# Ordering the last attention group by tile of queries, and starting each tile's output, norm and logits among the rest

## What is computed

```python
q, k, v = (split_heads(x @ W + b) for W, b in ((Wq, bq), (Wk, bk), (Wv, bv)))
attn = einsum('bhqd,bhkd->bhqk', q, k) / sqrt(32) + alibi        # causal mask
out = einsum('bhqk,bhkd->bhqd', softmax(attn), v) @ Wo + bo
x1 = layernorm(x + out)
logits = x1 @ Wr + br                                            # 4 experts, top 1
y = (silu(x1 @ Wg[e]) * (x1 @ Wu[e])) @ Wd[e] * top_w            # e: the expert of the token
result = layernorm(x1 + y)
```

## Time and profile before

| what | value |
|---|---|
| median of 3 runs | 1259.69 us (1257.77 to 1263.88) |
| the profiled execution | 1257.54 us, span 1255.8 us |
| PE busy | 1165.1 us, 93% of the span |
| DVE, ACT, POOL busy | 61%, 45%, 24% |
| first score of the last group (unit 180) | 451.13 us |
| last product with values (unit 191) | 483.97 us |
| o63 done | 486.37 us |
| routing starts on DVE | 509.53 us |

### The profile page before, as it was taken

One profiled execution on the slowest core, in us unless ns is written; L12 is line 12 of the kernel. 1 busy time (PEld: TensorE's weight loads), 2 busy tenths in 40 slices (PEclk: granted clock), 3 DMA queues, 4 the chain that ended last, 5 costly groups with the idle time before them and its releaser, 6 DMA issues.

```text
span 1255.8 us, 27816 instructions
## 1 busy us (share of the span) xinstructions
PE 1165.1 (93%) x8697; PEld 1063.2 (85%) x8697; DVE 768.6 (61%) x1978; ACT 570.4 (45%) x1395; POOL 307.3 (24%) x443
## 2 busy tenths in 40 slices
PE   6998998999899987499999999999999999999994
PEld 5888888887888875498998899899989988998993
DVE  3676767676767776456546655664665465456665
ACT  4676766765666673043323332332333232323344
POOL 5400201201020122353213311330331133123336
PEclk9999999999999998589999999999999999999997
DMA  8223223222322240271322223122313222231302
GB/s 274 62 52 79 71 67 103 54 60 68 94 52 64 68 123 35 61 200 44 93 68 62 75 79 91 51 85 68 93 51 91 72 60 76 72 98 51 85 33 103
DMA packets 109685, 100.11 MB, mean 80 GB/s; under 512 B 12847, under 2 KB 81839, under 8 KB 109552
## 3 DMA queue, kind: packets, MB, share of 16 engines
q1 hardware_dynamic: 104784, 87.85, 24.8%
q0 software_dynamic: 3040, 9.18, 2.2%
q10 hardware_dynamic: 1728, 1.31, 0.3%
HBM read 64.74 MB, written 9.18 MB: 59 GB/s over the span
## 4 chain that ended last, share of the span: by engine, by line
PE 76%; DVE 6%; POOL 5%; ACT 4%; issue 4%; DMA 3%; SPq 1%; ACTq 0%; DVEq 0%; POOLq 0%
PE bank L805 35%; PE bank L583 14%; PE bank L830 10%; PE bank L721 4%; PE bank L704 4%; POOL up_lo L1455 4%; PE bank L817 3%; PE bank L693 2%; DMA up_raw<-in_Wu_dram 2%; SPq L475 1%; ACT probs L913 1%; DVE probs L1153 1%; PE bank L730 1%; PE bank L681 1%; ACT up_hi L945 1%
## 5 line engine op out<-in xcount | busy, mean ns | idle before, releaser
L805 PE MATMUL bank<-up_hi,xsT_hi 128*128 x1216 | 356.2, 293 | 5.7 <-POOL up_lo L1455 4.6
L805 PE MATMUL bank<-up_lo,xsT_hi 128*128 x1216 | 344.6, 283 | 0.0
L805 PE MATMUL bank<-up_hi,xsT_lo 128*128 x1216 | 344.5, 283 | 0.0
L1455 POOL TENSOR_TENSOR up_lo<-up_raw,up_hi 128x256 fp32r<-128x256 f32 x241 | 169.9, 741 | 477.8 <-ACT up_hi L945 477.6
L1294 DVE SCALAR_TENSOR_TENSOR h_tok<-bank,row_weight,silu 128x128 f32<-128x128 f32 x304 | 93.4, 347 | 292.3 <-ACT silu L1009 292.3
L805 PEld LDWEIGHTS bank<-up_hi,xsT_hi 128*128 128x128 f32 x1216 | 233.0, 192 | 12.3 <-issue 12.0
L805 PEld LDWEIGHTS bank<-up_hi,xsT_lo 128*128 128x128 f32 x1216 | 233.7, 192 | 0.3
L805 PEld LDWEIGHTS bank<-up_lo,xsT_hi 128*128 128x128 f32 x1216 | 233.1, 192 | 0.0
L1009 ACT ACTIVATE silu<-bank 128x256 f32<-128x256 f32 (+1 forms) x160 | 59.6, 373 | 364.5 <-PE bank L805 364.5
L1311 DVE TENSOR_TENSOR y<-bank,y 128x512 f32<-128x512 f32 x295 | 198.5, 688 | 0.5
L913 ACT ACTIVATE probs<-probs,neg_max 128x512 f32<-128x512 f32 (+3 forms) x256 | 136.5, 558 | 56.4 <-DVE neg_max L1153 55.4
(11 more groups left out here) (168 smaller groups left out, 2083.8 us busy)
## 6 DMA issues: line engine op xcount, KB each, us to landing
up_raw<-in_Wg_dram SPq DMA_DIRECT2D x64, 256.0 KB, 3.5
up_raw<-in_Wu_dram SPq DMA_DIRECT2D x64, 256.0 KB, 4.1
down_raw<-in_Wd_dram SPq DMA_DIRECT2D x64, 256.0 KB, 2.7
k_stack<-qk_hi SPq DMA_DIRECT2D x128, 64.0 KB, 2.0
q_stack<-qk_hi SPq DMA_DIRECT2D x128, 64.0 KB, 2.0
k_stack<-qk_lo SPq DMA_DIRECT2D x64, 64.0 KB, 2.0
q_stack<-qk_lo SPq DMA_DIRECT2D x64, 64.0 KB, 2.0
x_tok<-in_x_dram SPq DMA_DIRECT2D x3, 1024.0 KB, 5.5
```

The source lines that it names most:

```text
L805: mm = pe.matmul(bank[:, n * 2 * P:(n + 1) * 2 * P], a[:, s, k, :], up_w[w][k][:, :, :].rearrange("p a f -> p (a f)")[:, bass.ds(at, 2 * P ...
L1455: pool.tensor_tensor(up_w[1][k][:, e, :], up_raw[:, idx % NUPS, k, :, :].rearrange("p g f -> p (g f)"), up_w[0][k][:, e, :].bitcast(F32), ...
```

## The change

The last group (heads 60 to 63) is no longer ordered by head but by tile of queries, in the order 2, 1, 3, 0. A "head" of that group now means one tile for all four heads: tile 2 is four units of 3 blocks, tile 1 two units of 4 blocks, tile 3 four units of 4 blocks, tile 0 one unit of 4 blocks. That makes 11 units instead of 12, with the same 40 blocks; `U` is 191. The first four units (180 to 183) each take another head's stack. Each `o6x` now completes one tile's rows, so `OT_last`, `OP_rest`, the norm and the logits of a tile become jobs of the plan, which runs on to unit 204 (`plan.units`) for them. `OT_last` is four jobs with 128 columns instead of one with 512. Two splits of expert weights on ACT (`split_up`), which stood behind the loop, go to units 195 and 196 (`UP_AT`). Up to unit 179 no instruction moves, and SP's list is the same throughout.

```diff
+TILE_ORDER = (2, 1, 3, 0)
+TILE_UNITS = {0: ((0, 1, 2, 3),), 1: ((0, 1), (2, 3)), 2: ((0,), (1,), (2,), (3,)), 3: ((0,), (1,), (2,), (3,))}
+UNITS = [(g, g * GH + h, [(h, i) for i in tiles]) for g in range(NG - 1) for h in range(GH) for tiles in UNIT_TILES]
+UNITS += [(NG - 1, (NG - 1) * GH + n, [(h, i) for h in heads]) for n, i in enumerate(TILE_ORDER) for heads in TILE_UNITS[i]]
...
+ROWS = list(range(T0)) + [T0 + i for i in TILE_ORDER]
...
+UP_AT = {U + VLAG + n: NUPS + n for n in range(NE - NUPS)}
...
+        if kind == "OT_last":
+            return [("o", DONE + LAST * NH + ROW[t] - T0), ("read", "OP", NT - 1)]
+        if kind == "x1t":
+            return [("ln", t)] + ([("read", "logit", ROWS[ROW[t] - 2])] if t >= T0 else [])
...
+                for job in list(queue) if u >= U else [queue[0]]:
+                    if all(k in ready for k in needs(job)):
+                        break
...
+                for t in ROWS[T0:]:
+                    queue.extend((kind, t) for kind in ("OT_last", "OP_rest", "x1t", "logit"))
...
-                if u % PER_HEAD == 0:
-                    pe.wait_ge(s_stack[h], stack_count(g))
+                for n, h, i, at, width in spans(pairs):
+                    if n == 0 and u % PER_HEAD == 0 and g < NG - 1 or g == NG - 1 and END[g * GH] >= u:
+                        pe.wait_ge(s_stack[h], stack_count(g))
...
-            head_values(NB * NH - 1)
-            for job in plan.after_loop + plan.tail:
-                side(job, 0, len(cost_of(job)))
...
-            for job in plan.after_loop + plan.tail[0:1 + QT]:
-                take(job)
-            for e in range(NUPS, NE):
-                split_up(0, e)
-            for job in plan.tail[1 + QT:]:
-                take(job)
+                if u in UP_AT:
+                    split_up(0, UP_AT[u])
...
-            for t in range(T0, NT):
-                take(("OP_rest", t))
-                moments(t)
-                if t > T0:
-                    normalise(t - 1)
-            normalise(NT - 1)
```

More of the change, by code:

```diff
@@ L98, in cost_of @@
             "OT": [53] * (3 if t // QT == LAST else 4), "OP": [213] * (9 if t // QT == LAST else 12),
[L99 removed]
+            "x1t": [53] * 4, "logit": [107] * 8, "OT_last": [53], "OP_rest": [213] * 3}[kind]
 class Plan:
@@ L106, in __init__, with next_bank, add @@
         self.number, self.bank, self.before, self.act_number = {}, {}, {}, {}
[L107 to L110, removed]
+        self.slices, self.taken_at = defaultdict(list), defaultdict(list)
+        self.moments_at, self.normal_at = {}, {}
         self.flushed = {}
         self.used = {}
[L114 to L118, removed]
+    def next_bank(self, banks):
+        return min(range(banks), key=lambda n: self.number.get(self.used.get(n), 0))
+    def add(self, job, bank):
+        self.number[job] = len(self.number) + 1
         self.bank[job] = bank
@@ L187, in owed @@
         return sum(c for _, c in left) + sum(sum(cost_of(j)) for j in queue)
-    for u in range(U + VLAG):
+    u = 0
+    while u < U + VLAG + 4 or queue or left or pending or later:
         flush(u)
+        if u == U:
+            for bank in range(2, 6):
+                plan.used.pop(bank, None)
         if u in SPLIT_BY:
@@ L541, in sync @@
             x_due = 2
-            for u in range(U + VLAG):
+            for u in range(plan.units):
                 if x_due <= NB and plan.flushed.get(("OP", (x_due - 2) * QT + QT - 1), U + 9) <= u:
@@ L697, in unit_transpose @@
             def unit_transpose(u):
-                blocks = sum(i + 1 for i in UNITS[u][2])
                 bank = banks[2 + u % 2]
@@ L1214, in step @@
                 dve.wait_ge(s_route, steps[0])
-            dve.wait_ge(s_side_dve, done("logit", NT - 1))
+            dve.wait_ge(s_side_dve, max(done("logit", t) for t in range(NT)))
             step(dve.tensor_reduce(mx, logits[:, :, :], AX_X, ALU.max))
```

211 lines of the change are left out of this document (102 added, 109 removed).

## The result

The changed kernel takes 1263.9 us (median of 20 runs, 1259.35 to 1268.38), the kernel before 1260.91 us in the same measurement (20 runs, 1257.77 to 1264.52). The ratio is 1.0027, with a 95% interval of 1.0014 to 1.0039: slower by 2 to 5 us, and less than the 0.5% that I called a difference. The forecast was 1264.5. It came so near the 1263.9 partly by luck: it was built on the 1259.69 us of three runs, and the 20 runs put the kernel before 1.2 us higher. The difference was forecast as 4.9 us, and the medians differ by 3.0.

What follows compares the result with a forecast made beforehand. Behind the last product, latency of a chain through all engines was the bound. A walk through the queues gave +1.7 + 9.1 − 5.2 = +5.6 us, or +4.3 if the clock returned; +4.9 gave 1264.5 us, range 1258.0 to 1268.5.

Steps and rivals of the forecast that it cites:

- Term 1: Up to the last product with values: PE waits for the fourth stack at unit 183, partly offset by fewer units; +1.7 us.
- nothing takes this back: Behind the stack wait at unit 183, ACT and then PE are full, so every later point stays 2.8 us later.
- The 1.1 us that I credited to eleven units instead of twelve: Up to the last product with values: 11 units leave fewer holes on PE, a gain of 1.1 us against the stack wait.
- Term 2: From the last product to o63: heads 62 and 63 queue behind steps of tiles 14 and 13; +9.1 us.
- Term 3: From o63 to the routing: two tiles left instead of four, but one after the other; 17.95 instead of 23.16, −5.2 us.
- heads held back more than the tail is shortened: The forecast itself, for the stretch up to the routing: fixed queues make it +4.3 to +5.6 us; chance 0.68.
- +5.6 case: The sum up to the routing if PE stays at the low clock from 488 us on: +5.6 us.
- middle value of 4.9: Routing start: middle of +5.6 us (low clock throughout) and +4.3 us (clock back at 493, lost again at 497.5).
- Gaps filled: Behind the last product: gaps are filled and the last heads are not held back; −3.5 us, 1256.2 us; chance 0.12.
- Low clock earlier: Holes on PE from 480 us bring the low clock earlier; +6.8 to +7.5 us, 1266.5 to 1267.2 us; chance 0.14.
- Stack absorbed: The fourth stack lands by 457 us and its wait is absorbed; +2.4 us, 1262.1 us; chance 0.06.
- if the stack lands earlier: Sign that the forecast is wrong: the fourth stack's DMA lands earlier than 3.2 us after its issue, forecast at 458.84.

Runs made afterwards that it cites:

- e7: The changed kernel with the four up_raw loads issued on POOL's queue instead of SP's, no split moved; 1267.4 us, ratio 1.0041 to the kernel before.
- e2: The changed kernel with the last group's row work from unit 194 on four units later, same order, so heads 62 and 63 pass first; 1267.8 us, ratio 1.0073.
- e4: The changed kernel's units with row work reordered: tile 14 starts early, other tiles' steps fill its waits; 1253.0 us, ratio 0.9945 to the kernel before.
- e3: The changed kernel's units, with all row work behind the last head, step by step over the four tiles; 1260.2 us, ratio 0.9996 to the kernel before.
- e6: The changed kernel with 31 filler matmuls that nobody reads ahead of the row products on PE; 1262.6 us, ratio 1.0019 to the kernel before.
- e8: e4 with the up_raw loads issued on POOL's queue; 1249.5 us, ratio 0.9914 to the kernel before.
- e10: The same program as e8, profiled and timed a second time; 1250.7 us, ratio 0.9933 to the kernel before.

## Why the prediction was right

**Term 1, +1.7 us, measured +0.45** (33.07 − 32.62, from 485.72 − 452.65 and 483.75 − 451.13). The last product ends at 485.95, close to the forecast 485.65, only because unit 180 started 1.5 us later in this execution. The place and the releaser were as forecast; both numbers in the term were too large. The stack wait: I took the DMA's 3.2 us of the earlier trace rows for the changed kernel too, and it landed in 2.0 us. The Trainium skill (DMA: Bandwidth & Descriptors, Anatomy of one DMA) gives about 2.0 us of fixed cost; here the changed kernel's trace agrees, with 2.0 us, and this row of before, with 3.2, does not. But the page of before's profile, which I had read, has 64 such DMAs with a median of 2.0 us:

```profile
q_stack<-qk_lo SPq DMA_DIRECT2D x64, 64.0 KB, 2.0
```

In the eleven executions that followed, the fourth stack landed in 2.0 to 2.4 us. So the 3.2 was the odd one, and one row was no safe price for a landing. My sum for that rule was wrong too: a landing at 457.8 instead of 458.84 takes 1.0 us off the wait, not 1.7. The step "nothing takes this back" was wrong as well: in e7 1.14 us of the wait went, and only 0.5 reached the last product. The 1.1 us that I credited to eleven units instead of twelve are hardly there: 32.58 against 32.62.

**Term 2, +9.1 us, measured +8.4.** From the end of the last product (485.95) to POOL's last `o_tok` done (496.77) are 10.82 us, in before 2.40. Head 62's transpose came 3.97 us behind the last product's end (forecast 4.78, from 485.65 to 490.43), head 63's 6.13 (6.90). The queueing was as forecast. It was shorter because the clock fell only in the course of 488 to 490 us (0.72), where I had it low from 488: tile 14's four transposes took 0.63 us there instead of my 0.86.

**Term 3, −5.2 us, measured −5.1.** 514.85 − 496.77 = 18.08 us, in before 23.16. The copies of 128 columns that the trace of before lacked take 0.28 us on ACT and 0.26 to 0.29 on DVE, at the nearest rows and well inside my bounds.

**What these two terms mean** I had only half right. As a sum they hold: the heads did wait, and where I said. But the name that I gave the cause, "heads held back more than the tail is shortened", is refuted by e2: with the heads let through, term 2 falls by 7.4 us (489.89 − 486.45 = 3.44 from the last product's end) and term 3 grows by 8.4 (516.35 − 489.89 = 26.46). Tile 15 doesn't ask for o63 at all but for o62, done at 494.18, and stands behind `logit` of tile 13 on PE (497.76 behind 496.06 to 497.9). Only tile 12 asks for o63, done at 496.77, and its transpose comes at 500.44. What costs is what the walk did step by step and I didn't name: two tiles' chains one after another ahead of tile 15, and tile 12's moments behind tile 15's split (506.41, then 507.02), so that the four transposes spread over 21.75 us, against 10.4 in before (494.31 to 504.69).

**The clock.** I left open whether it would come back at 493; it fell to 0.72 at 488 to 490 and stayed at 0.50 up to the routing and beyond, so the +5.6 case of the sum was the one that happened. As measured, the sum is 0.45 + 8.42 − 5.08 = 3.8, the difference of the tail distances. My middle value of 4.9 is 1.1 off that: the overrated stack and queue (1.25 and 0.65 us too much) are only partly offset by the clock, which I had taken half way (0.7 too little). The time of 1264.5 came nearer still, but there the low start of 1259.69 helped.

**The sum against the time.** The profiled execution is 6.2 us longer (1263.74 against 1257.54), of which 1.5 lie ahead of unit 180 and 0.8 behind the routing; the medians of 20 runs differ by 3.0, and 0.0027 of 1260.9 are 3.4. POOL's last split ended at 514.58 and delayed nothing, as forecast.

**The rivals.** "Gaps filled": the heads were held back as forecast, so it did not happen in this kernel. The Trainium skill's advice that interleaving stretches with different limits may help (Perfetto Trace Analysis, Optimization Strategy) is not borne out here as the change does it, 1.0027, and is for e4, 0.9945: the same units, the row steps side by side. Mixing the tail's steps in does not help by itself; e3, which undoes the mixing, has 0.9996. "Low clock earlier": PEclk was 1.00 up to 488 us; it did not occur. "Stack absorbed": it had 0.06 and was the nearest to what happened with term 1, with the wait still seen. One of my own signs of being wrong came true, "if the stack lands earlier".

## What to carry to other kernels

In a tail where no engine is full, the worth of an order is the number of hand-overs that follow one another in the fixed queues. List each engine's queue and look for a step of chain B that stands behind the last step of chain A, though it was ready before: with the same work, tiles side by side took 8.8 us off the tail distance of before (a microsecond or two of it may be the clock), and tile after tile added 3.8. An item that comes late, like the last heads here, is only a cause if what waits for it isn't held by something else too; moving it alone, as in e2, tells. Before that, look whether the item is done long before it is used, as o62 and o63 were. A wait that the trace names is worth what remains at the next full engine (0.5 of 1.14 us), and a landing time from one row is a sample, not a price: the page's median of 64 was the better one.

## What the runs showed of the hardware

- The granted clock stayed at 1.00 while PE was idle from 486 to 488 us, and fell only behind that, to 0.72 and then to 0.50 (the level of 1.2 GHz) at 490 to 493, when PE was busy again for 2.77 of 3.00 us.
- In e3 and e6, where PE waited 1.60 and 2.30 us for a stack and was busy for 1.71 and 1.70 of 4.00 us (454 to 458), the granted clock was 0.50 (460 to 464) and 0.60 and 0.54 (458 to 462) behind it, with PE busy all the time. In the changed kernel, with a wait of 1.31 us and 2.69 of 4.00 us busy (456 to 460), it stayed at 1.00.
- The same program, in e8 and e10, had the two levels of the clock in the same stretch (0.50 and 1.00 at 487 to 490 us). The part behind the last product was 17.17 and 16.07 us.
- The last DMA of the fourth stack (64 KB, issued by SP) landed in 3.2 us in before and in 2.0 to 2.4 us in the eleven other executions (the one for the third stack in 3.9 us in e3), and the wait at unit 183 was 1.31, 1.21, 0.96 and 2.30 us in four kernels with the same instructions up to there.
- The start of unit 180 lay between 449.6 and 456.6 us in the twelve profiled executions, though these kernels hardly differ up to it. Distances between two marks are free of that, but not of chance: up to the last product they agree within 0.01 us in two executions of one program (e8, e10), behind it they differ by 1.1.
- Four 256 KB loads cost POOL 0.77 to 1.01 us each to issue and SP 0.51 to 0.58; POOL had the time, SP's queue had not.
